# Differential attention with an FP4 feed-forward gate: norm, quantisation and the turns of x moved, turns on the DMA queue

## The reference, cut to what matters

```python
xn = (x - mean) / sqrt(var + 1e-5)
qkv = xn @ Wqkv.T + b                 # 8 heads x 2 maps of q, 4 x 2 of k (D = 128), 4 of v (2 D wide)
p = softmax(q1 k1') - lam * softmax(q2 k2')          # causal, per head
o = p @ v; o = o * rsqrt(mean(o*o) + eps) * subln_w * (1 - LAMBDA_INIT)
s = o.reshape(B, S, 2048) @ out_w.T + out_b
g = silu(fp4(xn) @ fp4(weight).T + bias)             # fp4: blocks of 32, shared power-of-two scale
out = x + s * g
```

## Time and profile before

| | |
|---|---|
| median of the runs | 1780.74 us |
| the profiled execution's own time | 1780.72 us |
| its span (first to last instruction) | 1778.5 us |
| PE busy | 1569.9 us, 88% |
| DVE busy | 1237.2 us, 70% |
| ACT busy | 874.0 us, 49% |
| POOL busy | 737.3 us, 41% |
| mean granted TensorE clock | 0.963 |

### The profile page before, as it was taken

The page is one execution under the profiler, slowest core; times in us unless marked ns, Lnnn a source line. Parts: engine busy times, 40 slices in busy tenths (PEclk is TensorE's granted clock), DMA queues, the critical chain, the costliest instruction groups (busy, mean ns, idle before and its releaser), DMA issues.

```text
span 1778.5 us, 29365 instructions
## 1 busy us (share of the span) xinstructions
PE 1569.9 (88%) x9425; PEld 921.1 (52%) x9425; DVE 1237.2 (70%) x3213; ACT 874.0 (49%) x2514; POOL 737.3 (41%) x1442
## 2 busy tenths in 40 slices
PE   2657898998889988999889988899988998899998
PEld 2334554555554555555554555545555555555554
DVE  4668888548884588746885488845887478854782
ACT  4554555335653356434553356534564355533561
POOL 2214563236542464324642364424643246323243
PEclk9888999999899999999999998999989999899999
DMA  7302223332233222332233223322233222322342
GB/s 266 95 1 68 49 45 63 76 61 56 55 83 61 55 50 55 81 73 50 49 59 78 66 51 57 84 57 59 47 62 75 72 50 54 54 55 65 60 77 69
DMA packets 331980, 117.55 MB, mean 66 GB/s; under 512 B 312978, under 2 KB 313524, under 8 KB 331828
## 3 DMA queue, kind: packets, MB, share of 16 engines
q1 hardware_dynamic: 331828, 115.70, 29.9%
HBM read 31.74 MB, written 8.39 MB: 23 GB/s over the span
## 4 chain that ended last, share of the span: by engine, by line
PE 36%; DVE 28%; POOL 13%; issue 12%; ACT 10%; DMA 1%; POOLq 0%; SPq 0%; ACTq 0%; DVEq 0%
PE ps L456 11%; PE ps L458 11%; PE ps L457 11%; DVE ps L935 5%; DVE qkv L891 4%; DVE pp L947 4%; DVE ph L953 4%; ACT qkv L635 3%; ACT ph L670 3%; DVE coef L944 2%; POOL norm L1138 2%; POOL gate L1112 2%; ACT pp L662 2%; POOL qkv L1098 2%; POOL v L1110 1%
## 5 line engine op out<-in xcount | busy, mean ns | idle before, releaser
L456 PE MATMUL ps<-xT,wqkv 128*128 128x512 f16 x768 | 297.5, 387 | 26.4 <-DVE qkv L891 24.6
L670 ACT ACTIVATE ph<-pp,small 128x128 f16<-128x128 f32 (+3 forms) x256 | 143.3, 560 | 320.3 <-DVE pp L947 319.3
L457 PE MATMUL ps<-xT,wqkv 128*128 128x512 f16 x768 | 296.1, 386 | 0.0
L458 PE MATMUL ps<-xT,wqkv 128*128 128x512 f16 x768 | 295.7, 385 | 0.0
L935 DVE CUSTOM_DVE_ANT_0 ps<-ps,mask,ssc 128x384 f32<-128x384 f32 (+3 forms) x512 | 281.9, 551 | 6.1 <-PE ps L520 6.1
L891 DVE SCALAR_TENSOR_TENSOR qkv<-ps,bsc,qkv 128x512 f16<-128x512 f32 x192 | 142.8, 747 | 140.4 <-ACT qkv L635 140.4
L674 ACT ACTIVATE junk<-ps 128x256 bf16<-128x256 f32 x256 | 97.1, 379 | 261.2 <-PE ps L458 261.1
L456 PE MATMUL ps<-qkv,pT 128*128 128x256 f16 x640 | 182.0, 284 | 37.8 <-DMA pT<-ph 36.6
L1136 POOL TENSOR_TENSOR norm<-norm,sumsq 128x1 f32<-128x1 f32 x256 | 49.5, 193 | 389.8 <-ACT junk L674 389.6
L953 DVE SCALAR_TENSOR_TENSOR ph<-pp,small,ph 128x128 f16<-128x128 f32 (+3 forms) x256 | 174.1, 680 | 43.1 <-ACT ph L670 30.6
L456 PE MATMUL ps<-wout,heads 128*128 128x512 f16 x512 | 194.1, 379 | 3.6 <-DVE small L921 3.3
(11 more groups left out here) (146 smaller groups left out, 3441.9 us busy)
## 6 DMA issues: line engine op xcount, KB each, us to landing
...
pT<-ph SPq DMA_TRANSPOSE x256, 2.7
heads<-on SPq DMA_TRANSPOSE x256, 2.5
...
```

The lines of the kernel that those rows point to most:

```text
L456: mm(out, ah, bh, start=start and j == 0, stop=False)
L457: mm(out, ah, bl, start=False, stop=False)
L458: last = mm(out, al, bh, start=False, stop=stop and j == n - 1)
L670: run(ph[:, u, 0:w], pp[:, 0:w], ACT.Copy, scale=sigma).then_inc(ph_hi, 1)
```

## The change: what it does

1. **Turns of x, quantised x and the gate's weight** leave PE. The low and high half of x are made in SBUF (`x_hi` on ACT, `x_lo` on DVE, in steps 15, 17, 18, 19), and SP issues DMA transposes: two of x in each of steps 21 and 22, two of the quantised x in each of steps 9 and 10, one of the weight in each of steps 6 to 9 of batch 0. The set-up does the same for batch 0, between the fourth and the fifth load of weights on SP's queue.
2. **Quantisation** of a batch's x goes to steps 1 to 4 of that batch itself (all six operations of four tiles), that of the weight to steps 5 to 8 of batch 0. The x of batch 0 is no longer quantised in the set-up.
3. **Layer norm** goes to step 7 for all four tiles. POOL keeps mean and root and makes a bias; ACT applies scale and bias in one instruction (`layer_norm`).
4. **Fills**: no `xT`, `aT`, `wT`; `ffn` in steps 10 to 13 of every batch; `v` of group 2 in steps 15 and 16; group 3 in steps 16, 16, 17, 17, 18... as `(0, 1, 1, 2, 3, 3, 4, 5)` from step 16 on. Steps 14, 22 and 23 of a middle batch have no fill.
5. **combine** writes its sum over the scores in PSUM and not in `pp`; `p_hi` and `p_lo` read it there. `scores(n+2)` so waits for `p_lo(n)` and not for `combine(n)`, and the second exponential for `combine` and not `p_lo`. The coefficient is a `tensor_scalar` of one tensor and two pointers.
6. **Order**: the evacuation of an `out` fill moves on DVE into the next step, behind `p_lo`, and in that step ACT squares o after `p_hi`. POOL's `eps_of` is one instruction and comes before the gate and residual products. SP issues `transpose_p` first in its step; in steps 0 to 7 `transpose_o` is issued in pairs in even steps.

The lookahead constant `AHEAD` is 2, as the order before has it.

```diff
-NORM_STEPS = [9, 12, 15, 18]
-QUANT_STEPS = [12, 17, 23, 27]
-PREP_AT = [(0, 0), (0, 1)] + [(0, 1), (1, 1), (2, 1), (2, 2), (3, 2), (4, 2)]
+AHEAD = 2
+PH = 4 - AHEAD
+W_STEP = 5
+X_STEP = 5
+FFN_STEP = 10
+QUANT_AT = {(s + ds, slot): [(k + a, op) for a, op in ops] for s, k in ((1, 0), (3, 2)) for ds, slot, ops in (
+    (0, "maxima", [(0, 0), (0, 1), (0, 2), (0, 3)]),
+    (0, "projected", [(0, 4), (0, 5), (1, 0), (1, 1), (1, 2), (1, 3)]),
+    (1, "projected", [(1, 4), (1, 5)]))}
+NORM_AT = {7: range(NT)}
+X_SPLIT = {15: 0, 17: 1, 18: 2, 19: 3}
+X_TURN = {21: (0, 1), 22: (2, 3)}
...
-        at = range(STEPS) if g < 3 else (0, 0, 1, 1, 2, 3, 4, 5)
+        at = (None, PROJ_AT, PROJ_AT[:6] + (7, 8), (0, 1, 1, 2, 3, 3, 4, 5))[g]
...
-        first = STEPS if has_next else LAST_STEP
-        steps[first + 2 * k].append(("aT", 0, k))
-        steps[first + 2 * k + 1].append(("ffn", 0, k))
+        steps[FFN_STEP + k].append(("ffn", 0, k))
...
+            def transpose_x(n):
+                k = n % NT
+                sp.wait_ge(xh_lo, n + 1)
+                sp.dma_start_transpose(xT[:, :, :, k * P:(k + 1) * P].rearrange("p s a t -> p (s a) t"),
+                                       xh[k].rearrange("p s h -> p (s h)")).then_inc(xT_done[k], 16)
...
+                for k in X_TURN.get(s, ()) if b + 1 < B else ():
+                    sp.wait_ge(fill_done, fill_of("v", b, G - 1, k // 2) + 1)
+                    transpose_x((b + 1) * NT + k)
...
+                for k in {FFN_STEP - 1: (0, 1), FFN_STEP: (2, 3)}.get(s, ()):
+                    if k == 0:
+                        sp.wait_ge(q_done, (b + 1) * NT + (NT if b else 0))
+                    if k == 2:
+                        sp.wait_ge(res_free, 16 + 16 * b * NT)
+                    sp.dma_start_transpose(aqT[k], aq[:, k, :]).then_inc(aT_done[k], 16)
...
-                wait(pe, comb_done, n - 1)
+                wait(pe, ph_lo, n - 1)
...
+            def layer_norm(k, n):
+                act.wait_ge(centred, n + 1)
+                run(xin[:, k, :], xin[:, k, :], ACT.Identity, scale=rstd[:, n % NT, 1:2], bias=rstd[:, n % NT, 2:3])\
+                    .then_inc(xn_done, 1)
+            def x_hi(n):
+                act.wait_ge(xn_done, n + 1)
+                if n % NT == 0 and n:
+                    act.wait_ge(res_free, 16 + 16 * (n - NT))
+                    act.wait_ge(q_done, 2 * NT)
+                run(xh[n % NT][:, 0, :], xin[:, n % NT, :], ACT.Copy, scale=X_SCALE).then_inc(xh_hi, 1)
...
-                stt(out=coef[:, u:u + 1], in0=recip[:], scalar=neglam, in1=l1, op0=ALU.mult, op1=ALU.mult)\
-                    .then_inc(coef_done, 1)
+                ts(coef[:, u:u + 1], l1, recip[:], neglam, ALU.mult, ALU.mult).then_inc(coef_done, 1)
                 dve.wait_ge(coef_done, n + 1)
-                stt(out=pp[:, 0:w], in0=sc_ps[u][:, 1, 0:w], scalar=coef[:, u:u + 1], in1=pp[:, 0:w],
+                stt(out=sc_ps[u][:, 1, 0:w], in0=sc_ps[u][:, 1, 0:w], scalar=coef[:, u:u + 1], in1=pp[:, 0:w],
...
-                stt(out=ph[:, u, w:2 * w], in0=pp[:, 0:w], scalar=sigma, in1=ph[:, u, 0:w],
+                stt(out=ph[:, n % PH, w:2 * w], in0=sc_ps[u][:, 1, 0:w], scalar=sigma, in1=ph[:, n % PH, 0:w],
...
+            def x_lo(n):
+                dve.wait_ge(xh_hi, n + 1)
+                stt(out=xh[n % NT][:, 1, :], in0=xin[:, n % NT, :], scalar=X_SCALE, in1=xh[n % NT][:, 0, :],
+                    op0=ALU.mult, op1=ALU.subtract).then_inc(xh_lo, 1)
...
             for n in range(NSTEPS):
                 b, s = n // NS, n % NS
+                late = [f for f in PLAN[n - 1] if f.kind == "out"] if n else []
+                if n + AHEAD - 1 < NSTEPS:
+                    combine(n + AHEAD - 1)
+                if n + AHEAD < NSTEPS and not late:
+                    maxima(n + AHEAD, 1)
+                if n + AHEAD - 1 < NSTEPS:
+                    p_lo(n + AHEAD - 1)
+                for f in late:
+                    fill(f)
+                if n + AHEAD < NSTEPS:
+                    if late:
+                        maxima(n + AHEAD, 1)
+                    maxima(n + AHEAD, 0)
+                prepare(b, s, "maxima")
                 if n:
                     normalised_lo(n - 1)
                 for f in PLAN[n]:
+                    if f.kind != "out":
+                        fill(f)
+                prepare(b, s, "projected")
+                if s in X_SPLIT and b + 1 < B:
+                    x_lo((b + 1) * NT + X_SPLIT[s])
```

More of the change, by code:

```diff
@@ L127, in plan @@
                 out = 4 * b + (j if kind == "last" else j - NT)
-                row.append(Fill(kind, g, j, n, hi, v, ffn, gate, out))
+                bank = held if kind == "last" and g else 1 - (bank if held is None else held)
+                row.append(Fill(kind, g, j, n, hi, v, ffn, gate, out, bank, used[bank]))
+                if kind == "last":
+                    held = bank if LAST_PIECES[j][g][1] < OC else None
+                used[bank] = n
                 n += 1
-                hi += kind in ("q", "k", "xT")
+                hi += kind in ("q", "k")
                 v += kind == "v"
@@ L133, in plan @@
             rows.append(row)
-    return rows[0], rows[1:], n
-FIRST, PLAN, FILLS = plan()
+    end = []
+    for k in (NT - 2, NT - 1):
+        bank = 1 - bank
+        end.append(Fill("out", 0, k, n, 0, 0, 0, 0, (B - 1) * NT + k, bank, used[bank]))
+        used[bank] = n
+        n += 1
+    return rows[0], rows[1:], end
+FIRST, PLAN, END = plan()
 assert len(FIRST) % 2 == 0
-END = [Fill("out", 0, k, FILLS + k - (NT - 2), 0, 0, 0, 0, (B - 1) * NT + k) for k in (NT - 2, NT - 1)]
 NSTEPS = B * NS
@@ L164, in setup_order @@
 def setup_order():
-    order = [("w", n) for n in range(8)] + [("fill", i) for i in range(NT)]
-    i = NT
+    order = [("w", n) for n in range(8)]
+    i = 0
     for n in range(8, WB):
@@ L242, in build @@
         one = small[:, 43:44]
+        minusone = small[:, 44:45]
         oamax = small[:, 12:20]
@@ L463, in fill @@
                 kind, g, j = f.kind, f.g, f.j
-                wait(pe, fill_free, f.n - 1)
-                bank = fbank[f.n % 2]
+                wait(pe, fill_free, f.prev + 1)
+                bank = fbank[f.bank]
                 if kind in ("q", "k"):
@@ L555, in _ @@
                     pe.wait_ge(fill_free, len(PROLOGUE) - 2)
-                    scores(1)
+                    for a in range(1, AHEAD):
+                        scores(a)
                     continue
@@ L981, in _ @@
                 elif kind == "ahead":
-                    combine(0)
-                    maxima(1, 1)
-                    p_lo(0)
-                    maxima(1, 0)
+                    for a in range(1, AHEAD):
+                        combine(a - 1)
+                        maxima(a, 1)
+                        p_lo(a - 1)
+                        maxima(a, 0)
                 elif kind == "w":
```

371 lines of the change are left out of this document (172 added, 199 removed).

## The result

The changed kernel takes 1754.5 us (median of 4 runs, 1752.72 to 1756.47) beside 1781.08 for the kernel before on the same chip: ratio 0.9855, 95% interval 0.9836 to 0.9875. It is faster by 27 us. The forecast was 77 (1704 us), so a third of it came. The time is inside the range (1658 to 1762), and equals rival B's 1754.

A forecast was written before the change was run, and what follows sets the result against it. It took PE to bind steps 0 to 7 and the circle DVE, ACT, DVE to bind steps 8 to 31. From 1780.72 us, 6 × -12.0 + 2.4 + 0 - 7 = -76.6 gave 1704 us, range 1658 to 1762.

The forecast's parts named there:

- rival B: Half given back: fills hold one another's banks, x's turn comes late; steps 8 to 31 take 127, kernel 1754 us; chance 0.17.
- The cover in steps 0 to 7: Output projections on PE leave DVE 39 us to spare; 19 us of moved quantisation and norm go in at no cost.
- The sum of DVE cycles as the pace of steps 8 to 31: In a middle batch DVE's cycles set the pace and sum to 120.6 us; PE's steps take 119.3 against 130.7.
- Steps 14 and 15: Middle batch: 8.6 us, minus a v evacuation, plus one x_lo, less the stall of p_lo, gives 8.1 us.
- PE's own work "not added": Turns of 3.2 and about 1.6 us a batch leave PE; not counted as gain, since PE is not the bound there.
- The combine in PSUM, no change but the stalls: p_lo at 512 keys takes 0.75 us from PSUM as from undisturbed SBUF; bounds -0.3 and +0.1 us a step.
- Stalls already in the sums: Coefficient and p_lo, with one tensor in SBUF, no longer stall beside POOL, x_lo may; nothing further added to the cycle sums.
- scores wait for p_lo, cost nothing: scores(n+2) waiting for p_lo(n) leaves 1.5 us spare in a 4.6 us cycle; between 0 and 1 us per stretch.
- Batch 0, net +2.4: First batch: steps 0 to 7 grow by 15.9 us to 66.8, steps 8 to 31 fall by 13.5 to 122.5.
- C: Rival, slower: PE's clock holds at 1.2 GHz through six fills from step 24 on; 1810 us; chance 0.06.
- A: Rival, down to the floor: DVE's stalls and ACT's lateness shrink more than counted, steps 8 to 31 take 113; 1654 us; chance 0.13.
- D: Rival, nothing gained: the wait only changes its name; 1781 us; chance 0.04.

The follow-up runs named there:

- e12: The changed kernel with the combined p back in SBUF and the coefficient and waits as before the change; 1747.4 us against the changed kernel's 1754.5.
- e13: The changed kernel without the transposing DMAs of p, attend reading a constant tile and waiting for p_lo alone; 1720.9 us.
- e14: The changed kernel with a second, small transposing DMA that nobody reads issued ahead of each transposition of p; 1804.5 us.

## Why the prediction was wrong

Right in sign, with a gain three times too large. Of the 50 us by which the forecast was too low, 29 are the six middle batches (199.8 for 195.0), 18 batch 0, and the rest batch 7 and the set-up. Point by point:

- *The cover in steps 0 to 7*: right. 75.3 us, and DVE's gaps are filled.
- *The sum of DVE cycles as the pace of steps 8 to 31* (120.6): the step that failed. Its terms for steps 8 to 13 and 25 to 29 were right (batch 3's cycles of 9 to 13 sum to 28.8 against 28.6 in the forecast, 25 to 29 to 24.7 against 24.6), steps 16 to 20 took 27.5 against 29.1 (group 3's fills stand in steps 16, 17, 17, 18 and so on, as the tuple in part 4 has it, and not in 16, 16, 17, 17, 18). Steps 14 and 15 took 11.7 against 8.1, steps 21 to 24 19.3 against 17.2, steps 30 and 31 8.2 against 7.7, and PE left 0.7 us later. (PE enters 0.4 after DVE, as the prediction says of batch 7, and its 119.3 is reckoned so; "before" in that sentence is a slip.) The step took it that less work on DVE is less time. e12 has 31.6 us more of it than the changed kernel and is no slower. In steps 21 to 24 the round of p is the pace: e13 shows that its DMA leg is worth 4.9 us of each middle batch, of which steps 23 and 24 have 4.4, and e14 that more of it costs more. Without it the middle batches take 194.9, where the forecast had 207.0 - 12.0 = 195.0; that they agree is luck, since it is made up otherwise: 14 and 15 stay long and 21 to 24 fall below the forecast (14.9 for 17.2). I had the latency as a bound ("no less than 3 us for each step without fill") and took its low end, without asking what stands behind attend on PE: the scores of three steps later.
- *Steps 14 and 15* (8.1): wrong by 3.6, the largest miss of a term, and not by the DMA (e13). p_lo and the normalised half come late from ScalarE (DVE waits 1.02 and 2.10 for it); that it is the tanh ahead of them was read from the timeline, not tried, and why these steps are long stays open.
- *PE's own work "not added"*: right, and of the 4.8 removed only 2.5 show in PE's busy time of batch 3 (189.4 to 186.9), while steps 14 and 15 now run at a clock of 0.71 and 0.74 (before, 14 to 21 had 1.00).
- *The combine in PSUM, no change but the stalls*: right for the duration. p_lo takes 0.751 from PSUM and 0.755 from SBUF, so the difference between the fixed terms for PSUM and SBUF sources that the Trainium skill gives in "VectorE: DVE Perf Modes" (on the TRN2 errata) isn't seen here. *Stalls already in the sums*: right that nothing was to be added. The coefficient takes 0.27 in each of its 256 places, not the 0.22 of the sign, which was the other instruction undisturbed. That this part alone was worth as much as the whole change I hadn't seen. The Trainium skill's "SBUF — State Buffer" (who interferes with whom), whose second half is of instructions outside the two-port modes alone, fits in both: with two SBUF inputs p_lo took 1.041 in the mean and up to 1.805, with one 0.751 in the mean and never more than 0.752.
- *scores wait for p_lo, cost nothing*: 1.7 us in batch 3; e12 puts the whole part at 0 to 7 us over the kernel.
- *Batch 0, net +2.4*: wrong by 18. Steps 0 to 7 took 66.2 (forecast 66.8), but by luck: the 66.8 is a sum of DVE cycles, and these took 75.9. DVE fell 9.7 us further behind PE meanwhile (0.8 at step 0, 10.5 at step 8), and steps 8 and 9 paid for it. Steps 8 to 31 took 141.3 against 122.5. I had given them a middle batch's time, whose DVE comes out of covered steps with no lag; here the round waits of the quantisation, DVE's for POOL's rounding, lie bare (about 1.7 us each, 6.7 in steps 0 to 7), and steps 8 and 9 have a clock of 0.71. From step 10 on the time is a middle batch's. I took DVE's sum as PE's.
- *Set-up, -7*: right (-5.7). *Batch 7, 0*: 2.4 more; e14 adds 7.6 there, so it feels the latency, but e13 takes off only 1.0: open.
- *Rivals*: B's time came, by other causes (steps 8 to 31 took 124.9 for its 127, batch 0 +20.6 for its +6). C's mechanism is there in small (a clock of 0.87 and 0.79 in steps 23 and 24, 1.00 in 25 to 31). A and D fell.
